# A fused graph layer on one core: indicator ahead of message on VectorE, one attribute block per chunk, destination offsets as bytes

## What is computed

```python
filt = silu(edge_attr @ Wf1 + bf1) @ Wf2 + bf2      # 100000 x 20 -> 256
msg  = xn[dst] * filt                                # gather by dst, which is sorted
agg  = segment_sum(msg, src)                         # scatter by src, which is random
```

## Time and profile before

| | |
|---|---|
| three runs | 2301.31, 2307.29, 2310.48 us; median 2307.29 |
| the profiled execution | 2302.29 us, its span 2300.5 us |
| opening | 0 to 188 us of the span |
| message stage, first to last scatter | 212.5 to 1783.2 us |
| the blocks behind it | 1783 to 2300 us |
| busy over the span | PE 84%, DVE 69%, POOL 64%, ACT 59% |

### The profile page before, as it was taken

One profiled execution on the slowest core, in us unless ns is written; L12 is line 12 of the kernel. 1 busy time (PEld: TensorE's weight loads), 2 busy tenths in 40 slices (PEclk: granted clock), 3 DMA queues, 4 the chain that ended last, 5 costly groups with the idle time before them and its releaser, 6 DMA issues. The chain is left out here.

```text
span 2300.5 us, 41215 instructions
## 1 busy us (share of the span) xinstructions
PE 1925.9 (84%) x10226; PEld 1592.2 (69%) x10226; DVE 1593.9 (69%) x3624; ACT 1353.8 (59%) x2428; POOL 1464.5 (64%) x991
## 2 busy tenths in 40 slices
PE   4686899889888988898889888988897486899878
PEld 3465677767766776677677767776776365688668
DVE  6555777777767776777677767777775467899745
ACT  2333766676667666666666666667665364566423
POOL 2122887788788877887788778878887460355400
PEclk9898999999999999999999999999999796899979
DMA  8656888988898889888888898889887881000002
GB/s 293 276 227 175 155 148 147 180 155 150 143 179 149 152 144 176 157 146 147 172 155 149 144 171 159 149 142 181 152 149 123 244 285 55 1 0 0 20 19 94
DMA packets 306121, 337.28 MB, mean 147 GB/s; under 512 B 35430, under 2 KB 269399, under 8 KB 305808
## 3 DMA queue, kind: packets, MB, share of 16 engines
q0 software_dynamic: 112896, 102.81, 37.8%
q1 hardware_dynamic: 187088, 227.31, 32.2%
q10 hardware_dynamic: 5888, 4.40, 0.8%
HBM read 179.32 MB, written 155.07 MB: 145 GB/s over the span
## 5 line engine op out<-in xcount | busy, mean ns | idle before, releaser
L911 POOL DMA_INDIRECT sums<-summed,out_idx x784 | 1261.3, 1609 | 334.3 <-issue 178.8
L966 PE MATMUL bank<-wf,hidT 128*128 128x256 f32 x3136 | 791.1, 380 | 0.0
L966 PEld LDWEIGHTS bank<-wf,hidT 128*128 128x128 f32 x3136 | 541.0, 190 | 52.6
L1057 ACT ACTIVATE hidT<-bank,bf 128x512 f32<-128x512 f32 x392 | 269.4, 687 | 447.8 <-PE bank L944 446.3
L1182 DVE TENSOR_TENSOR msg<-bank,gathered 128x512 f32<-128x512 f32 x392 | 271.1, 692 | 353.7 <-PE bank L966 340.9
L954 PE MATMUL bank<-window,spread 128*128 128x256 f32 x784 | 205.5, 344 | 198.4 <-DVE spread L1146 186.2
L954 PEld LDWEIGHTS bank<-window,spread 128*128 128x128 f32 x784 | 121.9, 189 | 297.0 <-DVE spread L1146 187.5
L1151 DVE TENSOR_TENSOR msg_low<-msg,msg_high 128x512 fp32r<-128x512 f32 x392 | 271.5, 693 | 48.4 <-ACT msg_high L1076 22.5
L964 PE MATMUL bank<-gnn_bf_halves,ones 128*128 128x256 f32 x784 | 295.8, 377 | 0.0
L1083 ACT ACTIVATE gathered<-bank 128x512 f32<-128x512 f32 x392 | 232.6, 593 | 51.9 <-PE bank L954 49.3
L1076 ACT ACTIVATE msg_high<-msg 128x512 fp32r<-128x512 f32 x392 | 246.9, 630 | 20.2 <-DVE msg L1182 19.7
(11 more groups left out here) (327 smaller groups left out, 2847.5 us busy)
## 6 DMA issues: line engine op xcount, KB each, us to landing
window<-xn_halves SPq DMA_DIRECT2D x392, 128.0 KB, 3.6
sums<-gate SPq DMA_DIRECT2D x32, 800.0 KB, 10.0
src_row<-id_rows SPq DMA_DIRECT2D x98, 256.0 KB, 4.5
dst_row<-id_rows SPq DMA_DIRECT2D x196, 128.0 KB
part<-sums SPq DMA_DIRECT2D x48, 512.0 KB, 6.0
attr<-attr_T SPq DMA_DIRECT2D x588, 40.0 KB
xn_halves<-xn_halves SPq DMA_DIRECT2D x7, 1792.0 KB, 6.5
sums<-summed,out_idx POOLq DMA_INDIRECT x784
```

The source lines that it names most:

```text
L911: nc.gpsimd.indirect_dma_start(g.sums_dram[k], bass.IndirectOffsetOnAxis(ap=out_idx[:, ET * c + t:ET * c + t + 1], axis=0), summed[c % 2][ ...
L966: mm = T.matmul(out, hidT[:, j // 2, f, ds((2 * (j % 2) + t) * P, P)], g.wf2[:, f, :], start=False, stop=f == CB - 1)
L1057: A.activation(hidT[:, h, f, :], hps[:], ACT.Silu, bias=g.bf1[:, f:f + 1]).then_inc(hid_ready, 1)
```

## The change

1. **Order on DVE.** In each step `indicate(j+2)` now stands ahead of `message(j)`.
2. **Attributes.** The host lays out one block of 128 rows by 512 for each chunk: both halves, three copies of each, zeros between. One DMA of 256 KB loads it, double-buffered by chunk, at j = 0. `high_attr` and `low_attr` run once in a chunk, on 128 and on 40 partitions (20 before, for each of two halves). The weights get matching rows for either half, put there by six small SBUF to SBUF DMAs at the end of SP's list of the opening, with a wait behind them.
3. **Destination offsets.** The opening subtracts each step's least destination on DVE and stores the difference, capped at 255, as bytes. The message stage loads 1,024 bytes by broadcast, one DMA of 128 KB for each chunk, two chunks ahead. `indicate` becomes a `tensor_tensor` of those bytes with `half_f`, broadcast along the row, in place of a `tensor_scalar` of int16 numbers with a column of `window_row`. PE's transposes, the cast and store of `dst` in int16, `window_row` and the broadcast of the ends go away.
4. **Places.** `load_src` moves from j = 0 to j = 3. POOL no longer clears `attr`.

```diff
-SPAN = 2 * 32 + EF
+ATTR_HIGH = ((0, 20), (40, 104))
+ATTR_LOW = (64, 84)
+LOW_ROWS = slice(64, 64 + 2 * EF)
+ID_BYTES = 3 * EC
+FAR = 255.0
...
+    wf1_zero = sb("wf1_zero", [P, 2, C], F32)
...
+    src16 = wide_f(e_node)[0:NCH, EC:EC + EC // 2].bitcast(I16)
+    offset = wide_f(e_col)[0:NCH, 0:EC]
+    offset8 = wide_f(e_col)[0:NCH, EC:EC + EC // 4].bitcast(U8)
...
+            sp.dma_start(wf1_raw[:], g.w["gnn_Wf1"]).then_inc(wf1_in, 16)
             sp.dma_start(src_i, g.src_cols).then_inc(cols_in, 16)
             sp.dma_start(g.dst_all[:], g.dst_cols).then_inc(cols_in, 16)
-            sp.wait_ge(cleared, CLEAR_WF1)
-            for copy in range(3):
-                sp.dma_start(wf1_raw[32 * copy:32 * copy + EF, :], g.w["gnn_Wf1"]).then_inc(cols_in, 16)
...
+            sp.wait_ge(wf1_ready, 4)
+            for h in range(2):
+                for rows, part in ((ATTR_HIGH[h][0], wf1_high), (ATTR_HIGH[h][1], wf1_low), (ATTR_LOW[h], wf1_high)):
+                    sp.dma_start(g.wf1_parts[rows:rows + EF, h, :].bitcast(F32), part[:].bitcast(F32)).then_inc(wf1_out, 16)
+            sp.wait_ge(wf1_out, 96)
...
-            for k in range(2):
-                pool.wait_ge(ids_in, 32)
-                G.tensor_copy(ids16[k], ids[k]).then_inc(filled, 1)
+            pool.wait_ge(ids_in, 32)
+            G.tensor_copy(src16, ids[0]).then_inc(filled, 1)
...
-            pe.wait_ge(win_step, 1)
-            for t in range(ET):
-                mm = T.transpose(g.ps[6 + t // 4][0:NCH, ds(t % 4 * P, P)],
-                                 dst_w.rearrange("p (c t) -> p t c", t=ET)[:, t, :], g.ident[:])
-            mm.then_inc(win_turned, 1)
...
-            act.wait_ge(filled, FILL_IDS)
-            for k in range(2):
-                act.dma_start(g.ids16_dram[:, k * EC:(k + 1) * EC], ids16[k]).then_inc(ids_out, 16)
+            act.wait_ge(filled, FILL_SRC)
+            act.dma_start(g.ids_dram[:, 0:2 * EC], src16.bitcast(U8)).then_inc(ids_out, 16)
...
+            act.wait_ge(offset_step, OFFSET_STEPS)
+            act.dma_start(g.ids_dram[:, 2 * EC:ID_BYTES], offset8).then_inc(ids_out, 16)
...
-            dve.wait_ge(cols_in, 80)
-            V.tensor_copy(dst_w, g.dst_all[:]).then_inc(win_step, 1)
+            dve.wait_ge(cleared, CLEAR_WF1)
+            V.tensor_copy(g.wf1_parts[:], wf1_zero[:]).then_inc(wf1_ready, 1)
+            dve.wait_ge(ids_in, 32)
+            dst_in = ids[1].rearrange("c (t e) -> c t e", e=PC)
+            V.tensor_reduce(extremes[:, 0, :], dst_in, X, ALU.min).then_inc(win_step, 1)
+            V.tensor_reduce(extremes[:, 1, :], dst_in, X, ALU.max).then_inc(win_step, 1)
+            dve.wait_ge(win_step, 2)
+            V.tensor_scalar(extremes[:, 0, :], extremes[:, 0, :], float(NPAD - HALF), None, ALU.min).then_inc(win_step, 1)
+            dve.wait_ge(win_step, 3)
+            V.tensor_tensor(extremes[:, 1, :], extremes[:, 1, :], extremes[:, 0, :], ALU.subtract).then_inc(win_step, 1)
+            V.tensor_tensor(offset.rearrange("c (t e) -> c t e", e=PC), dst_in,
+                            extremes[:, 0, :].unsqueeze(2).to_broadcast([NCH, PAIRS, PC]), ALU.subtract).then_inc(offset_step, 1)
+            dve.wait_ge(offset_step, 1)
+            V.tensor_scalar(offset8, offset, FAR, None, ALU.min).then_inc(offset_step, 1)
...
-            dve.wait_ge(win_turned, 1)
-            for k in range(2):
-                turned_dst = g.ps[6 + k][0:NCH, :].rearrange("c (t e) -> c t e", e=PC)
-                here = ds(2 * k, 2)
-                V.tensor_reduce(extremes[:, 0, here], turned_dst, X, ALU.min).then_inc(win_step, 1)
-                V.tensor_reduce(extremes[:, 1, here], turned_dst, X, ALU.max).then_inc(win_step, 1)
-            dve.wait_ge(win_step, 5)
-            V.tensor_scalar(extremes[:, 0, :], extremes[:, 0, :], float(NPAD - HALF), None, ALU.min).then_inc(win_step, 1)
-            dve.wait_ge(win_step, 6)
-            V.tensor_tensor(extremes[:, 1, :], extremes[:, 1, :], extremes[:, 0, :], ALU.subtract).then_inc(win_step, 1)
+            dve.wait_ge(wf1_in, 16)
+            V.tensor_copy(wf1_high[:], wf1_raw[:]).then_inc(wf1_ready, 1)
+            dve.wait_ge(wf1_ready, 2)
+            V.tensor_tensor(wf1_low[:], wf1_raw[:], wf1_high[:].bitcast(F32), ALU.subtract).then_inc(wf1_ready, 2)
...
+    attr = sb("attr", [P, 2, HE], F32)
+    attr_parts = sb("attr_parts", [P, 2, HE], F32R)
+    id_row = sb("id_row", [P, 2, ID_BYTES], U8)
...
-                sp.dma_start(src_row[:, p, :], g.ids16_dram[ds(c, 1), 0:EC].to_broadcast([P, EC])).then_inc(row_in[p], 16)
-
-            def load_attr(c, h):
-                for copy in range(3):
-                    sp.dma_start(attr[32 * copy:32 * copy + EF, h, :],
-                                 g.attr_T[:, ds(c * EC + h * HE, HE)]).then_inc(attr_in[h], 16)
-
-            def load_dst(c, h):
-                sp.dma_start(dst_row[:, h, :], g.ids16_dram[ds(c, 1), EC + h * HE:EC + (h + 1) * HE]
-                             .to_broadcast([P, HE])).then_inc(drow_in[h], 16)
+                sp.dma_start(id_row[:, p, 0:2 * EC], g.ids_dram[ds(c, 1), 0:2 * EC].to_broadcast([P, 2 * EC]))\
+                  .then_inc(row_in[p], 16)
+
+            def load_offsets(c, p):
+                sp.dma_start(id_row[:, p, 2 * EC:ID_BYTES], g.ids_dram[ds(c, 1), 2 * EC:ID_BYTES].to_broadcast([P, EC]))\
+                  .then_inc(offset_in[p], 16)
+
+            def load_attr(c, p):
+                sp.dma_start(attr[:, p, :], g.attr_rows[ds(c * P, P), :]).then_inc(attr_in[p], 16)
...
-                    if j == 0:
-                        if goes_on:
-                            sp.wait_ge(same_ready, PAIRS * (c + 1))
-                            load_src(c + 2, p)
-                        if not last:
-                            sp.wait_ge(spread_ready, PAIRS * c + 2)
-                            load_dst(c + 1, 0)
-                    if j == 1 and goes_on:
-                        sp.wait_ge(attr_ready, 2 * (c + 1) + 1)
-                        load_attr(c + 2, 0)
-                    if j == 2 and not last:
-                        sp.wait_ge(spread_ready, PAIRS * c + 4)
-                        load_dst(c + 1, 1)
+                    if j == 0 and goes_on:
+                        sp.wait_ge(attr_ready, c + 1)
+                        load_attr(c + 2, p)
+                    if j == 2 and goes_on:
+                        sp.wait_ge(spread_ready, PAIRS * (c + 1))
+                        load_offsets(c + 2, p)
                     if j == 3 and goes_on:
-                        sp.wait_ge(attr_ready, 2 * (c + 1) + 2)
-                        load_attr(c + 2, 1)
+                        sp.wait_ge(same_ready, PAIRS * (c + 1))
+                        load_src(c + 2, p)
...
                 load_src(p, p)
-            for h in range(2):
-                load_dst(0, h)
-            sp.wait_ge(attr_clear, 1)
-            for h in range(2):
-                load_attr(0, h)
+                load_offsets(p, p)
+                load_attr(p, p)
             for j in range(PAIRS):
                 load_window(0, j)
-            for h in range(2):
-                sp.wait_ge(attr_ready, h + 1)
-                load_attr(1, h)
...
-            nc.gpsimd.memset(attr[:], 0.0).then_inc(attr_clear, 1)
...
-            def high_attr(c, h):
-
-                act.wait_ge(attr_in[h], 48 * (c + 1))
-                if not is_first(c):
-                    act.wait_ge(hid_made, 4 * (c - 1) + 2 * h + 2)
-                A.activation(attr_parts[:, h, :], attr[:, h, :], ACT.Copy).then_inc(attr_rounded, 1)
+            def high_attr(i, p):
+
+                c = 2 * i + p
+                act.wait_ge(attr_in[p], 16 * i + 16)
+                if not is_first(i):
+                    act.wait_ge(hid_made, 4 * (c - 1))
+                A.activation(attr_parts[:, p, :], attr[:, p, :], ACT.Copy).then_inc(attr_rounded, 1)
...
-                    if j % 2 == 0 and not last:
-                        high_attr(c + 1, j // 2)
+                    if j == 0 and not last:
+                        high_attr(i + p, 1 - p)
...
-            def low_attr(c, h):
-
-                dve.wait_ge(attr_rounded, 2 * c + h + 1)
-                V.tensor_tensor(attr_parts[64:SPAN, h, :], attr[64:SPAN, h, :],
-                                attr_parts[64:SPAN, h, :].bitcast(F32), ALU.subtract).then_inc(attr_ready, 1)
-
-            def indicate(c, j):
-
-                if j % 2 == 0:
-                    dve.wait_ge(drow_in[j // 2], 16 * (c + 1))
+            def low_attr(c, p):
+
+                dve.wait_ge(attr_rounded, c + 1)
+                V.tensor_tensor(attr_parts[LOW_ROWS, p, :], attr[LOW_ROWS, p, :],
+                                attr_parts[LOW_ROWS, p, :].bitcast(F32), ALU.subtract).then_inc(attr_ready, 1)
+
+            def indicate(i, p, j):
+
+                c = 2 * i + p
+                if j == 0:
+                    dve.wait_ge(offset_in[p], 16 * i + 16)
```

(26 more changed lines are left out.)

74 lines of the change are left out of this document (31 added, 43 removed).

## The result

The changed kernel takes 2221.91 us (median of four runs, 2218.12 to 2224.21) against 2306.32 for the kernel before (four runs, one more than were shown ahead), a ratio of 0.9633 with a 95% interval of 0.9609 to 0.9657.

The account below looks back on a forecast made before the run. A ring of waits between PE and DVE was taken to set the pace, POOL next. Stage 783 x (1.62 + 0.306) + 15 + 8 = 1531 for 1570.7, -40; with opening and start -44, giving 2262 us, range 2228 to 2308.

Parts of the forecast that it names:

- The ring: Message stage: PE ends filt, DVE does message before indicator, PE waits to gather; 182.4 us of PE waits can go.
- under 20: Sign of being right: PE's wait at the gather for DVE's indicator falls under 20 us, from 182.4.
- POOL is the next bound: Message stage: POOL needs 3.83 us a step, 5% below the present 4.01; only its 71.3 us of waits can go.
- d: Mean duration of a scatter on POOL; 1.609 us before, forecast between 1.58 and 1.66.
- So the scatter stays near 1.61; I take 1.62: Message stage: mean surplus 0.073 us after the change, against 0.075 before by formula; bounds 1.54 and 1.74 us.
- 23 were left standing: Message stage, POOL's real waits: 15 us for earlier scatters plus 8 us of the others, of 71.3 before.
- The formula for random starts: Scatter's mean surplus over 1.54 us: sum of (duration - 0.13)^2 / 2 over a step's DVE instructions, divided by the step.
- rival A: Message stage: POOL and DVE fall into step, scatter 1.735 us, stage +42, 2345 us; chance with its like 0.12.
- rival C: Message stage: surplus shrinks with fewer low_attr and lucky phases, scatter 1.56 us, time 2203 us; chance 0.08.
- nothing on the path: Attributes per chunk: ACT saves 0.623 us and DVE 0.683, but both have slack, so no gain in time.
- B: Message stage: ring cut, 61 us of POOL waits stay; 2303 us, or 2275 with half won; chance 0.14 with D.
- D: Message stage: indicator still late through its wait for the gather two steps back; time as in B, joint chance 0.14.

Follow-up runs that it names:

- e1: Kernel before with only the indicator moved ahead of the message on DVE; 2240.34 us, ratio 0.9707.
- e6: Kernel before with the second of each step's two scatters left out, half of the sums missing; 2292.59 us in one run.
- e7: Kernel after with the second of each step's two scatters left out, half of the sums missing; 2138.67 us in one run.
- e10: Kernel after with the message written back to its PSUM bank, so msg_low has one SBUF input; 2212.01 us, ratio 0.9588.
- e4: Kernel after plus one unused DVE subtraction with two SBUF inputs in each chunk; 2228.51 us, ratio 0.9656.
- e5: Kernel after plus one unused DVE maximum with one SBUF input in each chunk; 2225.64 us, ratio 0.9656.
- e14: Kernel after with 256 KB instead of 128 KB loaded for a chunk's offsets, in one DMA; 2226.43 us, ratio 0.9654.
- e16: e13 with load_src moved from j = 0 to j = 3; 2232.87 us, ratio 0.9687.
- e3: Kernel after with the indicator as a tensor_scalar of the bytes with a column, one SBUF input; 2222.41 us, ratio 0.9637.
- e13: e8 with the indicator in its two-input form, on the old int16 rows; 2231.29 us, ratio 0.9673.
- e8: Kernel before with the new order and the new attribute block, destination numbers as before; 2232.76 us, ratio 0.9682.
- e17: e12 with the load of the offsets moved from j = 2 to j = 3; 2201.61 us, ratio 0.9554.
- e12: e10 with the six weight moves placed among SP's earlier work of the opening; 2207.96 us, ratio 0.9575.

## Why the prediction was right in kind and wrong in size

**The ring bounds the kernel, and the order cuts it: right.** e1 shows it for the order alone, e6 from the other side. PE's wait fell to 38.3 us where "under 20" was named as the sign: the cut is not clean, in 58 steps of 387 the indicator still came late, by 0.66 us in the mean. POOL hardly felt it: behind the first scatter its waits for `out_idx` sum to 4.2 us.

**POOL is the next bound, at 783 x (d + 0.306) and a few waits: right.** The real waits fell to 12 us, 18 scatters were in store at the end, and e7 and e10 show that less time on POOL shortens the stage. Other named signs came too: scatters nearly always behind "issue" (678 of 784, 585 before), idle time in the stage near 260 us (251.4), ACT's new wait for a landing (59.1), `low_half`'s rest above 60 us (126.5), an indicator at 0.42 and never held (404 to 479 ns, where some took 689).

**"So the scatter stays near 1.61; I take 1.62": this step failed.** The term d of the sum was mis-sized, by taking the scatters' starts as random. Measured 1.580, at the very edge of the 1.58 to 1.66 that the forecast named for d and below the sign's own bounds of 1.60 to 1.64. It is 783 x 0.040 = 31 of the 37 us by which the profiled execution (2221.5) beat the forecast for it (2258). The rest: real waits of 12 us where 23 were left standing (11 us), and against it the opening, the start and the blocks behind the stage, which gave +1.2 and not -4 (5 us). With d = 1.580 and all else as forecast the sum gives 2232 us by the median; the smaller waits took the time below 2228.

Why it failed can be said in part. The formula for random starts gave 0.075 before, and 0.069 was measured; that agreement was taken as support. Taken apart by place, the trace of before has no random starts: the first scatter of a step's pair has a surplus of 7 ns in the mean and the second of 130. The two halves happen to average 69, so the agreement was luck. In the kernel after the halves are 48 and 32, 40 in the mean, where the formula says 73; in e1 they are 69 and 64, near the formula's value. By instruction (the table above), every one of the four parts lies below its random value in the kernel after, and the largest gap is `msg_low`'s, 19.8 for 32.4 us. So which instruction of DVE stands at a scatter's start is a matter of phase, and the mean of 784 scatters hid it. The prediction did name the phase, as a danger (rival A, 0.12) and as luck (rival C, 0.08), but built the forecast on the random mean. That the rest of each two-input instruction is what costs is shown (e4, e5, e10); why the phases fall well with both data parts, and less well with each alone, was only narrowed down, by e14, e16, e3 and e13. Halving the number of `low_attr` is worth 0.010 us a scatter by the prediction's formula (0.038 / 3.85); e8 has 0.009 less inside `low_attr` and 0.006 more inside `msg_low`, 0.003 in all.

What of "nothing on the path" was said of attributes and offsets is right as far as waits go. It is wrong through d, and only where POOL is the bound: 17 us of stage with the order, and without it 6 us of time lost.

**The Trainium skill**, "SBUF — State Buffer", section "Who interferes with whom", says that a VectorE instruction with two SBUF inputs contends with a GpSimd instruction that reads SBUF. The pair e4 and e5 agrees with it, for scatters: 10.2 us of surplus for 98 two-input instructions, 0.2 for 98 one-input ones. By this rule the prediction made the indicator's new form dearer by up to 8 us; in the traces it is 2.8 us of surplus in the kernel after and 0.5 in e3, and the times differ by 0.5 us, within the uncertainty.

**The rivals.** A (phase lock, slower): no; the two halves are more even than before. B (nothing comes of the cut ring): no, the waits for `out_idx` went from 111.9 to 48.5 us, 44.3 of them ahead of the first scatter. D (the indicator late by its own wait for the gather two steps back): no, DVE waited for that gather once, for 2.4 us. C (the surplus shrinks to d = 1.56, 2203 us): the truth lies between it and the forecast, and the range leaves it out; e17 comes to its value by other means. Some of the prediction's small numbers don't come out: B with half of the waits won is 2272 or 2273 and not 2275, and the chances for "faster by more" sum to 0.77. Of SP's list, the prediction let the `attr_ready` wait go and did not count that a wait of the same length takes its place.

## What to carry to other kernels

Cutting a ring is worth what the next engine allows, and small savings on that engine begin to count only then: test such parts on top of the cut as well, for on the old kernel they read as nothing. When an engine's instruction has a spread of durations, split its mean by the instruction's place in the step before using it in a formula; a mean that agrees with "random" proves nothing about the phase. On a kernel bound by POOL's indirect DMAs, give DVE's long instructions one input in PSUM where that costs no bank.

## What the runs showed of the hardware

- A scatter (indirect DMA of 128 rows, issued by POOL) that starts inside a DVE instruction with two SBUF inputs is longer by the rest of that instruction less 0.13 us (1.86 for 1.54). With one SBUF input (a reduction, 0.46 us to go) or one input in PSUM (0.58 to go) it stays at 1.54. The old indicator, a block of SBUF compared with a column, is in between: with 0.20 us to go it lengthened the scatter to 1.61, and where it began 0.08 us before one, it took 0.40 us for 0.35 and the scatter 1.54.
- Two scatters in a row stand 0.306 us apart, in the kernel before and after alike, and never less than 0.303: "issue" has 0.307 each in the kernel after (208.3 / 678) and 0.306 before (178.8 / 585). It is 240 us of the stage.
- Six SBUF to SBUF DMAs of 20 rows took 1.3 to 1.4 us each in SP's list, where a 128 KB load of `id_row` takes 0.4 and the store of `gate_scale` 0.32. In an earlier place of the list (e12) they took as long, 1.28 to 1.44. The first scatter then came at 211.3 and 211.9 us (e12, e17); with the moves at the end it came between 211.2 and 213.4, so no gain is shown.
